# A fused slot-attention and top-1 expert kernel: first group's routing moved ahead of the second group's last step, fp32 dispatch, closing sums with tokens on partitions

## The reference, cut to what matters

```python
slots = layernorm(x)                       # h in the kernel
for _ in range(3):
    attn = softmax(q(rmsnorm(slots)) @ k.T, over slots); attn /= attn.sum(-1) + EPS
    updates = attn @ v
    r, z = sigmoid(xr + hr), sigmoid(xz + hz); n = tanh(xn + r * hn)
    slots = (1 - z) * n + z * slots
x = x + slots                              # x2 in the kernel
t = layernorm(x)
gates = softmax(t @ Wg); mask = one_hot(argmax(gates)); gate = sum(gates * mask)
pos = cumsum(mask, tokens) * mask - mask
dispatch = mask * (pos < capacity) * one_hot(pos, capacity)   # capacity 64
expert_inputs = einsum('bnd,bnec->becd', t, dispatch)
out = gelu(expert_inputs @ W1) @ W2                            # per expert, H = 512
x = x + einsum('becd,bnec->bnd', out, dispatch * gate)
```

## Time and profile before

| what | value |
|---|---|
| median of 3 runs | 138.56 us (138.42 to 139.27) |
| the profiled execution's own time | 138.64 us |
| its span, first to last instruction | 136.9 us |
| TensorE busy | 124.2 us, 91% |
| VectorE, ScalarE, GpSimd busy | 93.6, 79.4, 33.6 us |
| TensorE's share of the chain that ended last | 71% |

### The profile page before, as it was taken

One profiled execution on the slowest core, in us unless ns is written; L12 is line 12 of the kernel. 1 busy time (PEld: TensorE's weight loads), 2 busy tenths in 40 slices (PEclk: granted clock), 3 DMA queues, 4 the chain that ended last, 5 costly groups with the idle time before them and its releaser, 6 DMA issues.

```text
span 136.9 us, 2770 instructions
## 1 busy us (share of the span) xinstructions
PE 124.2 (91%) x1038; PEld 89.0 (65%) x1039; DVE 93.6 (68%) x304; ACT 79.4 (58%) x154; POOL 33.6 (25%) x54
## 2 busy tenths in 40 slices
PE   6999988999899998998978997699999999999950
PEld 2573843664664754754834943599999799987830
DVE  2797656996996996996997899974782041134751
ACT  1568383945855865765636678863694265315350
POOL 7633805005005005005000060027000065550000
PEclk9999999999999999999999999999999999999998
DMA  3989991000000000000000000000101201113115
GB/s 98 277 226 333 366 382 51 0 0 7 0 0 0 0 5 0 0 2 0 5 0 0 0 0 0 0 5 0 41 5 38 77 24 30 34 31 87 34 42 153
DMA packets 9197, 8.05 MB, mean 59 GB/s; under 512 B 601, under 2 KB 7028, under 8 KB 9184
## 3 DMA queue, kind: packets, MB, share of 16 engines
q1 hardware_dynamic: 8492, 7.28, 16.6%
q0 software_dynamic: 256, 0.40, 1.2%
q10 hardware_dynamic: 436, 0.20, 0.6%
HBM read 6.43 MB, written 1.57 MB: 58 GB/s over the span
## 4 chain that ended last, share of the span: by engine, by line
PE 71%; DVE 14%; ACT 9%; issue 3%; POOL 1%; ACTq 0%; DVEq 0%
PE ps L1302 11%; PE ps L1288 11%; PE ps L1144 6%; PE ps L1117 6%; PE ps L1136 5%; PE ps L1110 5%; PE ps L980 3%; PE ps L1314 3%; PE ps L1218 3%; ACT r_b L422 3%; PE ps L1063 3%; PE ps L1181 2%; PE ps L1093 2%; ACT z_b L436 2%; PE ps L1074 2%
## 5 line engine op out<-in xcount | busy, mean ns | idle before, releaser
L1144 PE MATMUL ps<-attn,VW 32*128 32x256 f32 x144 | 12.9, 426 | 3.5 <-DVE ps L712 2.0
L1288 PE MATMUL ps<-h,W_t 128*128 128x128 f32 x128 | 15.9, 279 | 0.0
L1288 PEld LDWEIGHTS ps<-h,W_t 128*128 128x128 f32 x128 | 15.0, 192 | 0.5 <-issue 0.3
L429 ACT ACTIVATE ps<-ps,half_b 128x512 f32<-128x512 f32 x12 | 7.9, 660 | 12.7 <-PE ps L1117 12.7
L1136 PE MATMUL ps<-h,whhT 128*128 128x256 f32 x48 | 13.7, 405 | 0.0
L1117 PE MATMUL ps<-h,whhT 128*128 128x256 f32 x48 | 13.3, 398 | 0.0
L346 POOL DMA_INDIRECT y_tok<-y_rows,row_of x8 | 8.3, 1034 | 18.9 <-DMA y_rows<-y_sb 14.1
L1144 PEld LDWEIGHTS ps<-attn,VW 32*128 32x128 f32 x144 | 5.6, 182 | 10.6 <-DVE ps L712 4.4
L1110 PE MATMUL ps<-h,whhT 128*128 128x256 f32 x48 | 11.7, 384 | 0.0
L422 ACT ACTIVATE r_b<-ps,half_b 128x512 f32<-128x512 f32 x12 | 7.6, 684 | 7.1 <-PE ps L1144 7.1
L712 DVE SCALAR_TENSOR_TENSOR ps<-r_b,ps 128x512 f32<-128x512 f32 x12 | 7.8, 693 | 5.1 <-ACT r_b L422 5.1
(11 more groups left out here) (168 smaller groups left out, 255.2 us busy)
## 6 DMA issues: line engine op xcount, KB each, us to landing
W_t<-in_L_ffn_W_dram SPq DMA_DIRECT2D x1, 2048.0 KB, 9.6
x_tok<-in_x_dram SPq DMA_DIRECT2D x4, 256.0 KB, 3.9
out_dram<-h SPq DMA_DIRECT2D x4, 256.0 KB, 2.3
y_rows<-y_sb SPq DMA_DIRECT2D x4, 128.0 KB, 1.8
n_b<-in_L_xattn_gru_whh_dram SPq DMA_DIRECT2D x1, 192.0 KB, 4.1
n_b<-in_L_xattn_gru_wih_dram SPq DMA_DIRECT2D x1, 192.0 KB, 3.5
y_tok<-y_rows,row_of POOLq DMA_INDIRECT x8, 3.7
n_b<-in_ctx_dram ACTq DMA_DIRECT2D x1, 64.0 KB, 2.9
```

Of the source, the lines that this page charges most:

```text
L1144: last = mm(to[:, hf, :], VW[g][p:p + M, gate * P:(gate + 1) * P], attn[g][p:p + M, :], start=False, stop=True, skip_group_check=True)
L1288: last = mm(hid_bank[e][:, j * BG * CAP:(j + 1) * BG * CAP], W1_t[:, ex_, j * P:(j + 1) * P], rhs, start=True, stop=True)
```

## The change

Half 4 now ends with `final_x(0)` and `final_x(1)` directly behind the `new_slots` of its batch, and group 0's `x2_back`, `x2_out`, `logits`, `x2_stats`, `choose`, `place` and `dispatch_hot` stand ahead of half 5's gates on TensorE, ScalarE and VectorE. Half 5's update gate is computed by `last_update` in the PSUM banks 4 and 5, the expert banks and `y_bank` change places, `attn_n` of half 5 comes behind `dispatch`, and `x_T(2)`, `x_T(3)` behind `up(1)`. `final_x` of group 1 reads the transposed x from PSUM. The fillers `keep_clock(2)` and `keep_clock(12)` are gone. `dispatch` multiplies the fp32 tokens once, block by block as each is ready, and `x_high`, `x_low` are gone. `combine` takes a 128x128 block of `comb` as the weight and `y_late` (fp32, one copy by ScalarE) as the moving side, so the sums have tokens on partitions, in two banks for each batch; `y_high`, `y_low`, `summed_out`, `back` and ScalarE's part of the last gating are gone. The last batch is written by two DMAs.

```diff
-        disp_bank = [bank[2], bank[3], bank[0], bank[1]]
+        disp_bank = [bank[6], bank[7], bank[0], bank[1]]
-        late_x_bank = [bank[1], bank[0]]
+        late_x_bank = [bank[4], bank[5]]
+        last_ZV = [ps[:, 4:6, NH:N], ps[:, 4:6, 0:NH]]
...
+            for k in range(2):
+                cs = slice(2 * k, 2 * k + 2)
+                sp.wait_ge(fin, C * (B - 1) + 2 * k + 2)
+                sp.dma_start(out[B - 1].rearrange("(c p) d -> p c d", p=P)[:, cs, :],
+                             res[:, B - 1, :].rearrange("p (c d) -> p c d", d=D)[:, cs, :]).then_inc(out_done, 16)
...
                 new_slots(g, 0, t)
+                if (g, t) == (0, ITERS - 1):
+                    final_x(0)
                 new_slots(g, 1, t)
+                if (g, t) == (0, ITERS - 1):
+                    final_x(1)
                 inv_denominators(og, ot)
...
+            def last_update(i):
+
+                g, t, b = NG - 1, ITERS - 1, batch(NG - 1, i)
+                if i == 1:
+                    pe.wait_ge(x2c, BG)
+                else:
+                    pe.wait_ge(S[g]["tz"], BG * t + 1)
+                for hf in range(2):
+                    mm(last_ZV[i][:, hf, :], whhT[:, P:2 * P], h[:, b, hf * NH:(hf + 1) * NH], start=True, stop=False,
+                       skip_group_check=True)
+                attn_gate(g, i, 1, last_ZV[i]).then_inc(S[g]["zp"], 1)
...
-                for part in (x_hi, x_lo):
-                    pe.wait_ge(xhi if part is x_hi else xlv, b + 1)
-                    for c in range(C):
-                        if part is x_hi:
-                            pe.wait_ge(dsp, b * C + c + 1)
-                        last = mm(disp_bank[b][:, :], part[:, b * C + c, :], disp[:, b % 2, c, :],
-                                  start=(c == 0 and part is x_hi), stop=(c == C - 1 and part is x_lo))
+                for c in range(C):
+                    n = b * C + c
+                    pe.wait_ge(dsp, n + 1)
+                    pe.wait_ge(x2ln, n + 1)
+                    last = mm(disp_bank[b][:, :], xln[:, n, :], disp[:, b % 2, c, :], start=(c == 0), stop=(c == C - 1))
...
-                    for part in (y_hi, y_lo):
-                        last = mm(acc_bank[i][:, :], part[:, s % 2, i, :], comb[s % 2][:, BG * g + i, :],
-                                  start=(k == 0 and part is y_hi), stop=(k == NP - 1 and part is y_lo))
+                    for c in range(C):
+                        last = mm(acc_bank[i][c // 2][:, c % 2 * D:(c % 2 + 1) * D], comb[s % 2][:, i, c * P:(c + 1) * P],
+                                  y_late[:, s % 2, i, :], start=(k == 0 and c % 2 == 0), stop=(k == NP - 1),
+                                  skip_group_check=True)
```

More of the change, by code:

```diff
@@ L159, in slot_attention_and_switch_ffn @@
         slot_r = sb("slot_r", [P, B * C], f32r)
[L160 to L163, removed]
+        disp = sb("disp", [P, 2, C, N])
+        comb = [sb(f"comb{k}", [P, BG, N]) for k in range(2)]
         y_sb = sb("y_sb", [P, NP, BG, D])
@@ L518, in _ @@
             t, g = ITERS - 1, NG - 1
+            x2_out(0)
+            x2_out(1)
             reset(g, 0, t)
@@ L558, in y_high @@
                     act.wait_ge(accP, s - NP - 1)
-                nc.scalar.activation(y_hi[:, s % 2, 0:BG, :],
+                nc.scalar.activation(y_late[:, s % 2, :, :],
                                      y_bank[s % 2][:, 0:BG * D].rearrange("p (b d) -> p b d", d=D),
[L561 to L567, removed]
+                                     ACT.Copy).then_inc(yl, 1)
+            update(g, 0, t)
+            candidate(g, 0, t)
             gelu(0)
-            x2_out(3)
+            candidate(g, 1, t)
             gelu(1)
             y_out(0)
+            x2_out(2)
+            x2_out(3)
             x2_norm(2)
             gelu(2)
-            x_high(2)
             x2_norm(3)
-            x_high(3)
             y_out(1)
@@ L812, in place, with dispatch_hot @@
                 v.tensor_copy(slot_r[:, cs], slot[:, cs]).then_inc(pl, 1)
-            def dispatch_hot(b):
+            def dispatch_hot(b, chunks=range(C)):
                 if b >= 2:
                     dve.wait_ge(xeP, b - 1)
-                for c in range(C):
+                for c in chunks:
                     v.tensor_scalar(disp[:, b % 2, c, :], slot_iota[:, :], slot[:, b * C + c:b * C + c + 1], None,
@@ L885, in _ @@
             place(0)
-            dispatch_hot(0)
+            dispatch_hot(0, (0, 1))
             x2_shift(1)
-            x_low(0)
+            dispatch_hot(0, (2, 3))
+            scale_logits(0)
             dispatch_hot(1)
-            scale_logits(0)
-            x_low(1)
+            reset_hn(g, 0, t)
+            reset_hn(g, 1, t)
+            kept_slots(g, 1, t)
+            kept_slots(g, 0, t)
+            gates(0)
+            weigh_n(g, 0, t)
             weigh_n(g, 1, t)
             new_slots(g, 0, t)
+            new_slots(g, 1, t)
             final_x(2)
-            new_slots(g, 1, t)
             final_x(3)
-            gates(0)
             def combine_hot(s):
@@ L1083, in exp_sums @@
                     pe.wait_ge(S[1]["h_ready"], 1)
-                mm(sum_ps, fold[:, :], esum[g][:, 0:1], start=(g == 0 and t == 0), stop=True,
+                mm(sum_ps, fold[:, :], esum[g][:, 0:1], start=(g, t) in ((0, 0), (NG - 1, ITERS - 1)), stop=True,
                    skip_group_check=True).then_inc(s["fold"], 1)
@@ L1270, in _ @@
             logits(1)
-            x_T(2)
-            x_T(3)
-            keep_clock(2, to=7)
+            attn_r(g, t)
+            last_update(1)
             positions(0)
-            keep_clock(12, to=7)
+            last_update(0)
             dispatch(0)
@@ L1312, in combine @@
                     pe.wait_ge(cmb, BG * k + i + 1)
[L1313 to L1329 removed]
+                    for c in range(C):
+                        last = mm(acc_bank[i][c // 2][:, c % 2 * D:(c % 2 + 1) * D], comb[s % 2][:, i, c * P:(c + 1) * P],
+                                  y_late[:, s % 2, i, :], start=(k == 0 and c % 2 == 0), stop=(k == NP - 1),
+                                  skip_group_check=True)
+                        if k == NP - 1 and c % 2 == 1:
+                            last.then_inc(accD, 1)
+                if k < NP - 1:
+                    last.then_inc(accP, 1)
             pe.wait_ge(w1_in, 16)
             pe.wait_ge(w2_in, 16)
[L1333 removed]
+            attn_n(g, t)
             pe.wait_ge(xeC, BG)
             up(0)
+            up(1)
+            x_T(2)
+            x_T(3)
+            down(0)
+            x2_back(2)
             x2_back(3)
[L1337 removed]
             logits(2)
             logits(3)
[L1340 removed]
+            up(2)
             positions(1)
[L1342 removed]
             down(1)
```

143 lines of the change are left out of this document (35 added, 108 removed).

## The result

The changed kernel is slower. The four executions took 143.26, 143.46, 147.01 and 148.11 us, with a median of 145.24, against a median of 138.87 us before (four executions; 138.56 was the median of three of them). The forecast was 140.3, slower, at most 143.0.

What follows compares the result with a forecast made beforehand. TensorE's full list was taken to bound 89.33 to 130.80 us, VectorE and handovers the stretch before. Terms -3.4 + 2.1 + 2.9 + 3.0 - 2.9 = +1.7 us on 138.64 gave 140.3 us, range 138.0 to 143.0.

Steps and rivals of the forecast that it cites:

- Step 1: Front, up to `up(0)`: attention later, group 0's routing earlier, `up(0)` at 85.9 instead of 89.33; -3.4 us.
- The forecast for cheap blocks: First dispatch: fp32 blocks at 0.48 us put `up(0)` near 82.9; as a rival 134.4 us in total, chance 0.08.
- Step 2: Behind `up(0)`: transposes and `x2_back(2)` moved into TensorE's full stretch, plus two short waits; +2.1 us.
- Step 3: Second dispatch: fp32 blocks take 6.8 instead of 3.85 us on a full TensorE, nothing hides it; +2.9 us.
- Step 4: Combine: each of four steps takes 1.87 instead of 1.13 us, bounds 0.95 and 1.87; +3.0 us.
- Step 5: End, behind the last combine: less gating and a smaller last DMA, 3.2 instead of 6.1 us; -2.9 us.
- The clock rival: TensorE's clock falls to 1.2 GHz from the stretch at 70 to 78 us, slowing dispatch; 143.7 to 147.1 us, chance 0.07.

Runs made afterwards that it cites:

- the split dispatch: The changed kernel with the earlier dispatch of two fp32r parts (x_high, x_low) put back; median 138.17 us, ratio 0.995 to the kernel before.
- the front alone: The changed kernel with the dispatch, combine and end of before, leaving the new front order; 138.05, 138.10, 140.83 and 140.90 us.

## Why the prediction failed

The direction was right, and the view of where the time is spent held: TensorE's list is full behind `up(0)`, and every us added to it was paid. The size was wrong: +1.7 us forecast for the span, +4.6 measured. Step by step:

- **Step 1, the front: right in its times, by luck in part.** `attention` started at 72.50 (forecast 72.8), the first dispatch at 78.40 (78.3), `up(0)` at 86.22 (85.9). -3.1 instead of -3.4 us. But what held the dispatch back was not the comparison, as forecast. The first comparison started at 77.29, 0.5 us earlier than the 77.8 of the forecast, and `last_update`, which I had hidden with 0.2 us to spare, ended at 78.46 and not at 78.1: each takes 1.76 us (1.13 + 0.63), not 1.2. The time came out right because `last_update`, 0.4 us late, ended where the comparison had been forecast to. The forecast for cheap blocks, `up(0)` near 82.9, was too low: the split dispatch reached 84.0, since the copy by ScalarE and the subtraction by VectorE stand between the layernorm and TensorE.
- **Step 2, what moved behind up(0): right in what it counted, and this is the step that failed.** The stage took 3.8 us more, not 2.1. Without the clock it is 2.3, so transposes, waits and order were as said, within 0.2 us. The other 1.5 us are the clock, which the sum had at nothing and which fell behind the instructions whose move this step counted. I had priced their length and not what a row of them can do to the price of their followers. That the row has a part in it is shown by the order alone, with `up(2)` in between (141.5 against 143.4) and by the fillers (142.5): of the executions with the row broken, 30 of 35 had a mean clock of 0.989 or more, of those with the row whole, 7 of 31. The row alone isn't enough. Of the six profiled executions with it whole three fell near 96 us (the changed kernel twice, and with the combine of before) and three held (the split dispatch, the front alone, the fillers in the front).
- **Step 3: right.** 7.06 against 6.8, 0.44 us an instruction, so the fp32 rows at 128 and 256 columns do tell the price at 512, and a little more than in proportion to my 0.42. The undone dispatch gave it back, 3.2 us.
- **Step 4: undersized by 0.3 us.** A combine step is 1.98 us, not 1.87; that it is the upper bound and not 0.95 was right.
- **Step 5: oversized by 0.3 us.** VectorE needs 0.9 us behind the last matmul, since its eight gatings form one piece and TensorE outruns them, and a half transfer isn't quicker. Steps 4 and 5 cost 0.7 us net, as undoing both showed.
- **The clock rival** had a chance of 0.07, a place (the front, behind 70 to 78 us) and a price (143.7 to 147.1). Two of the first four executions took 147.0 and 148.1. Neither was profiled, but two executions caught in like kernels show a fall at 74 to 75 us, one of 3 us and one of 10. So the place was right, and for the long executions of the changed kernel it is likely and not shown. Its chance was far too low, and I looked for one place only; the second, near 96 us, is what both profiled executions of the changed kernel have.

The reason for the low chance was a wrong reading. I took the earlier trace rows, a clock of 1.00 from 71.77 to 83.17, as evidence that transposes and 8-column matmuls leave the clock alone. In the kernel before they stand some 3.7 us in a row and then bf16 matmuls with 512 columns follow; with those taken out all nine executions have a mean clock of 0.965 to 0.970. The row can't show the absence of a risk, since the fillers covered it. Nor does that run by itself put the fall down to the row, as TensorE also stands idle for 3.2 us there. At group 1 the kernel before has `up(1)` between the last transposes and the 8-column matmuls, and its clock stayed at 1.00. The Trainium skill, "TensorE: Matmul & The Clock Gate", Part 4, has it that transposes don't count as busy in the same way for the clock gate. The traces agree with the direction of that sentence: TensorE was busy 1.01 of 1.26 and 1.94 of 1.94 us ahead of the fall near 96 us, and it fell nevertheless. They don't separate the transposes from the 8-column matmuls, nor both from the short waits.

Without any fall the change costs 141.7 (one execution) against 138.7, 3.0 us, of which the forecast had 1.7; the rest is 0.2 to 0.3 us each from the front, what moved behind `up(0)`, the second dispatch, the combine and the end.

What stays open: what, beside the row, decides whether the clock falls near 96 us; why it held there in four of six executions with fillers in the front alone; why the falls come in some executions and not in others of the same kernel; and why the first 10 us ran at half rate in some (139.2 of the split dispatch, 143.81 of the moved `up(2)`).

## What to carry to other kernels

A reordering that gains on paper can be paid for by a change of arithmetic that rides with it: here the new front with fillers is worth 1.3%, and the fp32 dispatch alone costs 5 us; time each alone before giving up on either. On a full TensorE, price plain fp32 by columns (0.44 us an instruction at 512, two for each product), and expect little from fp32r at 128 columns with a weight load for each instruction. A forecast of a start time is confirmed only when the chain goes through the instruction that was said to set it. A mean clock near 1 or a like mean clock in two executions doesn't say that they ran alike; look at the windows. When transposes and narrow matmuls are gathered in a row, or fillers are removed, read what stood behind them before, and spread wide matmuls between them.

## What the runs showed of the hardware

- The granted clock fell from 2.4 to 1.2 GHz with TensorE 96% busy by the profile (5.85 of 6.10 us from 90.0 to 96.1), behind transposes and 8-column matmuls. In other executions the same row left it at 2.4. It came back about 3 us later there, and about 10 us later in the profiled execution of 141.21, while wider matmuls ran.
- In the split dispatch's trace TensorE's instructions took twice their time until about 10 us (four transposes 0.85 instead of 0.44 us) while the recorded granted clock was 1.00.
- In the kernel before without its fillers the clock fell at about 82 us inside an idle stretch of 3.2 us (80.5 to 83.7), for some 7 us, in the profiled execution; the mean clocks of all nine (0.965 to 0.970) fit the same fall.
- A 128x128 by 128-column fp32r instruction with its own weight load took 0.121 us, fp32 0.124; at 512 columns fp32r took 0.24 and fp32 0.44 (7.06 / 16).
- A DMA of 128 KB from SBUF to memory behind another landed after 2.2 us, of 256 KB after 2.3.
